# Attention-side x tiles turned by VectorE through DRAM, and TensorE's side work moved behind the values of a step

## The reference

```python
x = L0_attn_q                                   # (8, 512, 256) f32: 4096 tokens of 256
xn = _layernorm(x, axis=-1)
x = x + attention(xn, k, v) + ffn(xn, ...)

# attention: b=8, s=512, 1024 keys
scale = q[:, ::step].reshape(b, -1)             # every 128th row gives the 1024 factors of the keys
qk = jnp.einsum('bsd,btd->bst', q, k)
softmax_qk = jax.nn.softmax(qk * scale[:, None, :], axis=-1)
return jnp.einsum('bst,btv->bsv', softmax_qk, v)

# ffn: a shared MLP 256 -> 1024 -> 256 for all tokens, and 8 routed experts of the same shape, top 2 of each token
logits = xf @ Wr
topk_p, topk_i = jax.lax.top_k(jax.nn.softmax(logits, axis=-1), 2)
routed = sum over e of (new_gelu(xf @ Wfc[e] + bfc[e]) @ Wproj[e] + bproj[e]) * gate[:, e:e + 1]
```

## Time and profile before

| | |
|---|---|
| median of 3 runs | 772.22 us (771.32 to 772.35) |
| the profiled execution | 772.56 us, its span 770.8 us |
| granted TensorE clock | 0.998 |
| TensorE busy (matmul) | 758.7 us, 98% of the span |
| VectorE, ScalarE, GpSimd busy | 468.6, 447.8, 230.1 us |

### The profile page before, as it was taken

How to read it: one execution, slowest core, us unless ns; L and a number is a source line. 1 busy time by engine, 2 the same in 40 slices (tenths; PEclk the granted TensorE clock), 3 DMA queues, 4 the chain that set the end, 5 groups by cost and what they waited for, 6 DMA issues and landing times.

```text
span 770.8 us, 21390 instructions
## 1 busy us (share of the span) xinstructions
PE 758.7 (98%) x6969; PEld 646.5 (84%) x6969; DVE 468.6 (61%) x1162; ACT 447.8 (58%) x862; POOL 230.1 (30%) x272
## 2 busy tenths in 40 slices
PE   6999999999999999999999999999999999999998
PEld 5789876777777777999899988888888888888887
DVE  5878858888887697454544544444344444336776
ACT  5567447666668775465646555555544555544452
POOL 2345425656566762012112121221221221210000
PEclk9999999999999999999999999999999999999999
DMA  9543222656566957665522557546465546304564
GB/s 308 203 140 97 98 83 74 210 205 229 210 208 208 331 219 263 199 171 128 166 69 69 161 156 219 173 122 218 123 181 160 177 131 205 97 28 148 161 205 151
DMA packets 104669, 129.19 MB, mean 168 GB/s; under 512 B 60240, under 2 KB 86192, under 8 KB 98208
## 3 DMA queue, kind: packets, MB, share of 16 engines
q1 hardware_dynamic: 79504, 106.20, 44.8%
q0 software_dynamic: 6480, 17.77, 6.2%
q10 hardware_dynamic: 18624, 4.46, 2.9%
HBM read 88.27 MB, written 40.13 MB: 167 GB/s over the span
## 4 chain that ended last, share of the span: by engine, by line
PE 93%; DVE 3%; issue 1%; POOL 1%; DMA 1%; ACT 0%; DVEq 0%; POOLq 0%; ACTq 0%
PE ps_v L1391 33%; PE ps_h L1371 32%; PE ps_v L1531 11%; PE ps_h L1467 11%; PE ps_t L1481 4%; DMA slots_x<-x_split,pos_i 1%; POOL slots_x L691 0%; PE ps_t L1320 0%; PE ps_v L1398 0%; PE ps_v L1320 0%; DVE h_split L988 0%; DVE v_split L1049 0%; DVE x_t L900 0%; ACT h L783 0%; DVE w_shared L1015 0%
## 5 line engine op out<-in xcount | busy, mean ns | idle before, releaser
L988 DVE TENSOR_TENSOR h_split<-h,h_split 128x512 f16<-128x512 f32 (+1 forms) x224 | 142.8, 643 | 161.1 <-ACT h_split L789 160.7
L783 ACT ACTIVATE h<-ps_h,b_fc 128x256 f32<-128x256 f32 (+1 forms) x320 | 125.7, 443 | 156.4 <-PE ps_h L1371 156.4
L1371 PE MATMUL ps_h<-x_t,w_split 128*128 128x256 f16 (+1 forms) x1920 | 193.3, 261 | 0.1
L1391 PE MATMUL ps_v<-w_stage,h_split 128*128 128x256 f16 x1704 | 192.6, 273 | 0.2 <-issue 0.2
L1371 PEld LDWEIGHTS ps_h<-x_t,w_split 128*128 128x128 f16 x1920 | 170.3, 98 | 17.4 <-issue 0.4
L1391 PEld LDWEIGHTS ps_v<-w_stage,h_split 128*128 128x128 f16 x1704 | 166.3, 98 | 19.4 <-issue 0.3
L727 POOL DMA_INDIRECT tokens_y<-prob,to_i x71 | 73.1, 1030 | 325.8 <-DMA tokens_y<-prob,to_i 181.6
L789 ACT CAST h_split<-h 128x512 f16<-128x512 f32 (+1 forms) x224 | 130.7, 584 | 10.1
L783 ACT ACTIVATE h<-ps_h,b_t 128x256 f32<-128x256 f32 x128 | 53.4, 467 | 62.2 <-PE ps_h L1371 59.1
L1531 PE MATMUL ps_v<-v_split,p_t 128*128 128x256 f16 x768 | 88.9, 273 | 0.0
L1467 PE MATMUL ps_h<-k_t,x_t 128*128 128x512 f16 x384 | 88.1, 380 | 0.0
(11 more groups left out here) (159 smaller groups left out, 600.1 us busy)
## 6 DMA issues: line engine op xcount, KB each, us to landing
w_split<-wpack SPq DMA_DIRECT2D x17, 1024.0 KB, 5.8
w_stage<-wpack SPq DMA_DIRECT2D x17, 1024.0 KB, 5.3
wpack<-w_split SPq DMA_DIRECT2D x8, 1024.0 KB, 5.0
wpack<-h_split SPq DMA_DIRECT2D x8, 1024.0 KB, 5.0
y_rows<-tokens_y SPq DMA_DIRECT2D x32, 256.0 KB, 3.3
b_pj<-bias_e SPq DMA_DIRECT2D x40, 128.5 KB, 3.2
w_stage<-in_L_ffn_Wfc_dram SPq DMA_DIRECT2D x4, 1024.0 KB, 7.2
scale_b<-key_scale SPq DMA_DIRECT2D x8, 512.0 KB, 7.3
```

Source lines behind the costliest of these rows:

```text
L783: ins = nc.scalar.activation(h32[:, hc, 0:n], ps_h[:, hc * TILE:hc * TILE + n], ACT.Gelu_apprx_tanh, bias=bias[:, hc:hc + 1], scale=1.0 / WS)
L988: ve.tensor_tensor(h_split[par][:, 1, 2 * b:2 * b + 2, 0:n], h32[:, 2 * b:2 * b + 2, 0:n], h_split[par][:, 0, 2 * b:2 * b + 2, 0:n], ALU.s ...
L1371: ins = mm(ps_h[:, hc * TILE:hc * TILE + cols], wv[:, wl, c, hc * P:(hc + 1) * P], x[:, xl * DC + c, 0:cols], start=n == 0, stop=n == 3 * ...
L1391: ins = mm(ps_y[a][:, :], h_split[par][:, xl, c, a * P:(a + 1) * P], wv[:, wl, c, :], start=n == 0, stop=n == 3 * HC - 1)
```

## The change

Tiles 9 to 15 are no longer turned by TensorE. When `x_split` of tile i is complete, SyncE stores it to a DRAM tensor `x_pass` (phase 1), and in phase 2 loads it back with four DMAs into the buffer of `xn`, each quarter of the columns to 32 partitions; VectorE turns it by one block transpose straight into `x_t` in phase 0 of the next round, between scale_scores and normalize. The copy from PSUM falls away. TensorE's `side_work(u)` now stands behind `values(u - 1)`. VectorE reads its results at the head of step u + 1, before finish. The tables of step 23 go to the head of step 24, those of step 24 to the tail of step 25.

```diff
+            def store_pass(i):
+                par = i % 2
+                if passed(i) > 1:
+                    wait_ge(sp, s_pass_in[par], 16 * QUADS * (passed(i) - 1))
+                wait_ge(sp, s_hl, 2 * i)
+                sp.dma_start(rows(x_pass, par * TILE, TILE), x_split[i % 3][:, :, 0:ROW]).then_inc(s_pass_out[par], 16)
+
+            def load_pass(i):
+                par = i % 2
+                wait_ge(sp, s_row_out[par], 16 * (i // 2 + 1))
+                wait_ge(sp, s_pass_out[par], 16 * passed(i))
+                for qd in range(QUADS):
+                    src = x_pass[par * TILE:(par + 1) * TILE, qd * QW:(qd + 1) * QW].rearrange("(b t) f -> t b f", t=32)
+                    sp.dma_start(xn_quad[par][qd * 32:(qd + 1) * 32, :, :], src).then_inc(s_pass_in[par], 16)
...
                 if phase == 1 and i < SHARED:
                     store_row(i)
+                    store_pass(i)
+                if phase == 2 and i < SHARED:
+                    load_pass(i)
...
                 if i >= 3:
                     act.wait_ge(s_scat[1 - par], 64 * ((i - 3) // 2 + 1))
-                    act.wait_ge(s_tr, i - 2)
+                    if i - 3 > NA:
+                        act.wait_ge(s_pass_out[1 - par], 16 * passed(i - 3))
+                    else:
+                        act.wait_ge(s_tr, i - 2)
...
-                if u == 23:
+                if u == 24:
                     dve.wait_ge(s_count, 1)
...
-                if u == 24:
+                if u == 25:
                     settle()
...
+            def turn_pass(i):
+                par = i % 2
+                dve.wait_ge(s_pass_in[par], 16 * QUADS * passed(i))
+                ve.transpose(x_t[:, i, :, :].rearrange("p c (b t) -> p b c t", t=32),
+                             xn_quad[par].rearrange("p b (r c) -> p b c r", r=32)).then_inc(s_xt, 1)
+
             for u in range(QT):
                 k, phase = u // 3, u % 3
                 i = NA + 1 + k
+                if phase == 1 and i - 1 < SHARED:
+                    front_a(route=i - 1, bank=side[(u - 1) % 2])
+                if phase == 2 and i - 1 < SHARED:
+                    front_b(route=i - 1, bank=side[(u - 1) % 2])
+                if u == 24:
+                    tables(u)
                 if u >= 2:
                     finish(u - 2)
                 p_lo(u)
                 if u + 2 < QT:
                     scale_scores(u + 2)
+                if phase == 0 and k and i - 1 < SHARED:
+                    turn_pass(i - 1)
                 if phase == 0 and i < SHARED:
                     front_b(norm=i)
                 if phase == 1 and i < SHARED:
                     front_b(split=i)
-                if phase == 0 and i - 1 < SHARED:
-                    front_a(route=i - 1, bank=side[u % 2])
-                if phase == 1 and i - 1 < SHARED:
-                    front_b(route=i - 1, bank=side[u % 2])
-                if phase == 2 and i < SHARED:
-                    copy_xt(i, bank=side16[u % 2])
                 if phase == 2 and i + 1 < SHARED:
                     front_a(stat=i + 1)
...
-                if phase == 2 and i < SHARED:
-                    tr1_side(i, u)
...
-                side_work(u)
                 if u:
                     values(u - 1)
+                side_work(u)
```

More of the change, by code:

```diff
@@ L90, in moe_attention_block @@
     wpack = dram("wpack", (EXPERTS * P, 4 * 2048), f16)
+    x_pass = dram("x_pass", (2 * TILE, ROW), f16)
     bfct_d = dram("bfct_d", (P, EXPERTS * HC), f32)
@@ L199, in moe_attention_block @@
                   for t in x_split[0:2]]
+        xn_quad = [t[:, :, :].rearrange("p a d -> p (a d)").bitcast(f16).rearrange("p (t n) -> p t n", n=QW) for t in xn]
         w_fc = w_split
@@ L215, in moe_attention_block @@
         side = [ps_v[:, a * 512:(a + 1) * 512] for a in range(2)]
-        side16 = [t.bitcast(f16) for t in side]
         def lg_ps(bank):
@@ L233, in moe_attention_block @@
         s_row_out = sem2("s_row_out")
+        s_pass_out = sem2("s_pass_out")
+        s_pass_in = sem2("s_pass_in")
         s_wproj_in = sem("s_wproj_in")
@@ L370, in x_half, with passed @@
             return x_split[i % 3][:, :, 0:ROW].rearrange("p a (f h c) -> p h a f c", h=2, c=DC)[:, hl]
+        def passed(i):
+            return (i - NA - 1) // 2 + 1
         def by_chunk(t):
@@ L1217, in _ @@
                     split_h(R0, 0, banks=(0, 1))
-                tables(u)
+                if u != 24:
+                    tables(u)
             finish(QT - 2)
@@ L1330, in tr1 @@
                 transpose_quads(x_split[i % 3]).then_inc(s_tr, 1)
-            def tr1_side(i, u):
-                pe.wait_ge(s_hl, 2 * i)
-                pe.wait_ge(s_fin, u - 1)
-                transpose_quads(x_split[i % 3], out=side16[u % 2]).then_inc(s_tr, 1)
             def router(i, bank=misc):
@@ L1491, in side_read @@
                     pe.wait_ge(s_rb, (i - 1) * RB + 2)
-                if phase == 2 and i < SHARED:
-                    pe.wait_ge(s_xt, i + 1)
                 if u == 23:
```

## The result

The changed kernel takes 777.5 us (median of 4 runs, 776.5 to 777.9), the kernel before in the same runs 772.25 (4 runs): ratio 1.007, 95% interval 1.0058 to 1.0082. It is slower by 5.3 us, and outside the range that was given. The profiled execution took 777.9 us with a span of 776.1, the granted clock was 0.993 over the span.

What follows compares the result with a forecast made beforehand. TensorE, busy 98%, was taken as the bound. The terms -3.15 + 3.2 - 0.78 + 0.3 + 0 gave -0.4 us, so 771.8 us against the median of 772.22; the range for 8 in 10 was 769.2 to 775.5.

Steps and rivals of the forecast that it cites:

- What bounds the kernel: Whole kernel: TensorE, busy 98% of the span, so a gain must take work or a wait from it.
- What the change removes: TensorE: 56 transposes go, eight for each of 7 tiles at 0.45 us a tile, -3.15 us.
- What it adds on the path: Phase-0 steps: the router waits 0.46 us for the tile turned behind scale_scores, seven times, +3.2 us.
- The first steps: Step 1: the values no longer stand behind the rank that waits for VectorE's front_a, -0.78 us.
- The rest of the front: Normalize behind the turn, its loop with GpSimd, and later front_a: all covered by slack, 0 us.
- just under the period: Loop from finish over GpSimd's split, scatter and inv_std to normalize: some 19.0 us against a three-step period of 19.03.
- The block transpose held by GpSimd: Rival, phase 0: GpSimd's L677 holds the transpose, router 1.9 us later in up to six tiles, 783 us; chance 0.05.
- The end of the stage: Steps 24 and 25: the scan hardly waits for GpSimd and the table is no later, taken as 0 us.
- SyncE's queue: Tile loads behind jobs: landing 10 to 14 us after phase 2 began against a limit of 11.2, taken as +0.3 us.
- upper bound of 8: SyncE's queue at worst: 2.6 us late for each of the three tiles behind a job, 8 us in all.
- the tiles land late: Rival, phase 0: late loads hold VectorE, router and TensorE; 774 us, up to 780 if three tiles pay 2.6; chance 0.18.

Runs made afterwards that it cites:

- e7: Kernel before, tiles still turned by TensorE; only the side work moved behind the values, its results read at the head of the next step: 771.67 us.
- e3: e1 with VectorE's block transpose of a phase-0 step moved ahead of scale_scores: 772.04 us.
- e1: Changed kernel with SyncE's jobs and scale load of a phase-1 step issued behind the tile's four loads, for all tiles: 771.43 us.
- e2: Changed kernel with only the scale load of step 10 issued behind tile 12's four loads, the job staying ahead: 775.06 us.
- e5: e1 with three more block transposes of tile 13 in step 15, each waited for, to make TensorE wait: 777.53 us.
- e9: Changed kernel with the tile's four loads issued from ScalarE's queue, SyncE's jobs left where they are: 804.13 us.
- e6: e1 with one more block transpose of tile 13 in step 15, waited for, to make TensorE wait: 773.28 us.
- e8: e3 with GpSimd's split of a phase-0 step made to wait for that step's normalize: 769.6 us.
- e11: e8 with SyncE's jobs held behind a tile's loads only in steps 4 and 10, no longer in step 16: 770.54 us.

## Why the prediction was wrong

- **What bounds the kernel**: right. Each difference lies in TensorE's steps and is read there.
- **What the change removes**: right. The phase-2 steps are 0.41 shorter; 0.45 went and 0.04 came by the step below. The figures of the Trainium skill's "VectorE: DVE Perf Modes", section "The three transpose paths", that were weighed there would have made it a gain of 21.8 us; nothing like it came.
- **What it adds on the path**: right. Block transpose at T + 5.14 for 1242 ns, 0.44 of wait for 0.46 that were taken. (The idle figure of 0.4 to 0.5 that was named as a sign reads 0.28, since it counts from a modelled end; the 0.44 is from start to start.) e7 and e3 show that it is this order and nothing else: without the turn, or with the turn earlier, the router has no wait.
- **The first steps**: right, 0.76 for 0.78 (e7: 0.77).
- **The rest of the front**: right for the loop, at 0, and e3 shows the "just under the period" to be no more than that. One cost was not seen: `transpose_probs` behind a router or a rank instead of behind the values takes some 0.03 to 0.04 longer, 14 to 16 times, which makes this term +0.5 to +0.6 (e7).
- **The block transpose held by GpSimd**: right to give it little. It runs 1.24 in step 9 with L702 beginning 0.53 into it. The section "Who interferes with whom" of the Trainium skill's "SBUF — State Buffer", by which it isn't held, agrees with this row; normalize in the same place is held again (1.97).
- **The end of the stage**: right, 0.18 for the scan, and no wait in step 30.
- **SyncE's queue: this step failed.** It was taken as +0.3, and measures 4.2: 3.96 in step 12 and 0.25 in step 18. The working had what stands ahead of tile 12's loads out of the way about 9 us after phase 2 began, and then 1 to 4.8 us for the loads themselves; of this it took the lower end, "since the loads' own time in the upper bound is mostly issue and latency, which overlap the job". The trace shows 10.1 and then 5.0: the first piece moved at 190.68 and the tile landed at about 195.7, although the loads had been queued since 184.43 to 186.78. So the landing came at 15.1 where 10 to 14 was given, and nothing of the loads' own time overlapped the job. Even with nothing ahead the 1024 pieces take 2.1 to 2.4 us (tile 9; tile 12 in e1), not the 1 us that came from their bytes; in step 12 they took 4.2. Pieces of GpSimd's scatter and of the next job's store moved in that time too, but which of them held up the loads isn't shown. e2 shows that the bytes ahead count in full (0.5 MB, 1.9 us). Tiles 10 and 14, with 0.5 MB less ahead, were in time and 0.16 us late. The upper bound of 8 was itself too high by its own terms: it took 2.6 us for all three tiles, where two of them were said to be 1.5 shorter, which makes 4.8. That the whole loss of 6.7 lies between 0 and 8 is luck.
- **The clock: a term that was missing.** A wait of TensorE of some us costs more than itself: 2.48 here, 1.7 in e2 and e5. With the 4.2 of the queue this makes the 6.7.
- **The rivals**: "the tiles land late" is what happened, at 777.5 within its 774 to 780, but through one tile of 3.96 and the clock behind it, not through three. That the time fell into the range of this rival, which had no term for the clock, is luck in part.

Without the queue's cost the sum is -0.7 us. e1 has -0.2 from step 0 to step 30, the 0.5 to 0.6 between them being the cost that was not seen, and -0.4 in the runs' medians (interval -0.9 to +0.5), so this part stands within what can be measured.

## What to carry to other kernels

A transfer that is needed soon and stands in one queue behind larger ones has to be priced with all bytes ahead of it, at the rate that the trace shows for full DMA engines, and with its own time on top (2 to 4 us here for 256 KB in small pieces); and where the result is near the limit, the place in the queue is the first thing to change; a queue of its own was much worse here. A lateness on the path of TensorE that grows to some us should be priced with the step at half clock behind it. A saving on the bounding engine comes out only when the loops just under the period (here GpSimd's and VectorE's) are shortened too: look for them before, as they are next.

## What the runs showed of the hardware

- In the attention stage the granted clock of TensorE went from 1.00 to 0.50 (2.4 to 1.2 GHz) around waits of 9.02, 8.96 and 6.47 (e9), 4.24 (changed), 4.12 (e5) and 2.35 us (e2), and not around one of 1.57 (e6), 1.26 (e3), 1.22 (e8), 1.14 (e9) or 1.01 (e11). The step behind took 1.4 to 2.5 us more. With 4.24, and in e9, the clock fell during the wait, with 4.12 and 2.35 only about 1 us behind it (at 217.25 in e5, 196.78 in e2). TensorE then worked at 0.50 for 5.3 us in the changed kernel and for 3.4 in e2 and e5, and the step was longer by about half of that.
- Loads of 64 KB in pieces of 256 bytes, with transfers of 1 MB in flight, landed in 7.0 us (median of 12) in the queue behind these, and in 13.3 us in another queue beside them, where pieces of 256 bytes and of 1 or 4 KB moved about one for one. With nothing ahead, the 1024 pieces of four such loads moved in 2.1 us.
- A `transpose_probs` (float32, eight matmuls) directly behind eight matmuls of 16 columns or five of 8 takes 0.90 to 0.91 us to the next start, behind matmuls of 256 columns 0.87 or 0.88.
- VectorE's block transpose of 128 x 1024 float16 takes 1235 to 1250 ns beside GpSimd's subtraction (six of the seven in the changed kernel), and 1246 without it, while normalize beside it takes up to 1.97 us there and 2.54 in e3, and 0.7 alone.
